# A fused decoder layer in fp32 split in two parts: packed order behind the chosen experts, a shared product ahead of the barrier, row numbers stored beside the routed tiles, another order of the attention steps

## The reference

```python
x = layernorm(x + attention(x))            # 16 heads of 32, causal, q k v and output projections with biases
x = layernorm(x + chosen(x, token_ids))    # 4 experts; the expert of a row is given by its token id:
                                           # y = (silu(x @ W[e].T) * (x @ W[e].T)) @ W[e].T, all three weights are ctx_2048
h = x @ Wr; probs = softmax(h); the two largest of 8 experts, weights not renormalised
moe = sum over the two of prob * (silu(x @ Wg[e]) * (x @ Wu[e])) @ Wd[e]          # F = 352
shared = sigmoid(x @ Wsg) * ((silu(x @ Sg) * (x @ Su)) @ Sd)                      # 1408 columns
out = layernorm(x + moe + shared)
```

## Time and profile before

| | |
|---|---|
| median of three runs | 1285.53 us (1281.93, 1285.53, 1288.90) |
| the profiled execution: its time, its span | 1281.12 us, 1279.4 us |
| PE busy, PEld busy | 1183.3 us (92%), 938.2 us (73%) |
| VectorE, ACT, GpSimd busy | 691.8 us (54%), 455.7 us (36%), 238.2 us (19%) |
| DMA | 169.72 MB, mean 133 GB/s |
| attention, until the first chosen load | 0 to 459.4 us |
| chosen experts | 459.4 to 597 us |
| routed phase | 597 to 1279.4 us |

### The profile page before, as it was taken

How to read it: one execution, slowest core, us unless ns; L and a number is a source line. 1 busy time by engine, 2 the same in 40 slices (tenths; PEclk the granted TensorE clock), 3 DMA queues, 4 the chain that set the end, 5 groups by cost and what they waited for, 6 DMA issues and landing times.

```text
span 1279.4 us, 20171 instructions
## 1 busy us (share of the span) xinstructions
PE 1183.3 (92%) x6404; PEld 938.2 (73%) x6404; DVE 691.8 (54%) x1469; ACT 455.7 (36%) x698; POOL 238.2 (19%) x358
## 2 busy tenths in 40 slices
PE   7788999999999769995999999999999999899996
PEld 5555566566576558884678888899999998678885
DVE  5664556656657546664547744444344432676754
ACT  3244334433435222221433334244444443333331
POOL 2021312412513410002300441000000000433200
PEclk8989999999999879997899999999999999999998
DMA  7355663532523322223523566344444531656440
GB/s 241 84 168 163 222 187 106 151 93 51 141 64 89 108 82 83 83 83 94 170 74 99 177 223 211 92 150 138 150 152 146 186 106 42 205 178 199 142 140 33
DMA packets 129276, 169.72 MB, mean 133 GB/s; under 512 B 17552, under 2 KB 70800, under 8 KB 129168
## 3 DMA queue, kind: packets, MB, share of 16 engines
q1 hardware_dynamic: 115360, 136.64, 34.7%
q0 software_dynamic: 8496, 28.32, 6.6%
q10 hardware_dynamic: 5312, 3.42, 1.1%
HBM read 95.98 MB, written 47.19 MB: 112 GB/s over the span
## 4 chain that ended last, share of the span: by engine, by line
PE 52%; DVE 4%; POOL 2%; issue 2%; DMA 2%; ACT 1%; SPq 0%; ACTq 0%; DVEq 0%; POOLq 0%
PE routed_ps L808 17%; PE routed_ps L1361 16%; PE chosen_psG L808 4%; PE chosen_psY L808 4%; PE routed_ps L1380 2%; PE routed_ps L1381 2%; PE routed_ps L1382 2%; POOL routed_rows_io L1299 2%; PE routed_ps L1402 1%; DVE routed_held L1704 1%; PE routed_ps L1425 1%; PE chosen_psX L889 1%; DMA routed_wdraw<-in_L_ffn_Wd_dram 1%; PE chosen_psH L908 1%; PE routed_ps L1326 1%
## 5 line engine op out<-in xcount | busy, mean ns | idle before, releaser
L459 PE MATMUL psT<-store 128*128 128x512 f32 x576 | 159.9, 412 | 5.1 <-DVE store L673 3.2
L742 DVE CUSTOM_DVE_ANT_0 psS<-psS,attn_mask 128x512 f32<-128x512 f32 (+3 forms) x256 | 120.6, 514 | 54.6 <-PE psS L525 54.5
L629 ACT ACTIVATE acc<-psE 128x512 f32<-128x512 f32 x160 | 92.9, 598 | 147.5 <-PE psE L546 143.5
L1361 PE MATMUL routed_ps<-routed_later,routed_held 128*128 128x512 f32 x528 | 124.7, 392 | 5.9 <-issue 2.9
L1361 PE MATMUL routed_ps<-routed_first,routed_held 128*128 128x512 f32 x528 | 127.6, 395 | 1.4 <-DVE routed_first L1800 1.4
L459 PEld LDWEIGHTS psT<-store 128*128 128x128 f32 x576 | 108.1, 198 | 26.0 <-issue 3.9
L1361 PEld LDWEIGHTS routed_ps<-routed_later,routed_held 128*128 128x128 f32 x528 | 98.3, 188 | 30.1 <-DVE routed_held L1704 6.6
L808 PE MATMUL routed_ps<-routed_held,routed_h_hi 128*128 x624 | 116.3, 328 | 0.6 <-DVE routed_h_lo L1745 0.6
L1361 PEld LDWEIGHTS routed_ps<-routed_first,routed_held 128*128 128x128 f32 x528 | 99.4, 190 | 22.1 <-DVE routed_first L1800 1.8
L1299 POOL DMA_INDIRECT routed_rows_io<-sorted_y,routed_pos x32 | 37.5, 1173 | 388.1 <-DMA sorted_y<-routed_rows_io 314.3
L402 POOL TENSOR_SCALAR_AFFINE_SELECT acc<-acc 128x256 f32<-128x256 f32 (+1 forms) x160 | 56.9, 361 | 282.8 <-ACT acc L629 281.9
(11 more groups left out here) (248 smaller groups left out, 1980.1 us busy)
## 6 DMA issues: line engine op xcount, KB each, us to landing
sorted_x<-attn_zero SPq DMA_DIRECT2D x19, 768.0 KB, 4.7
routed_sraw<-in_L_ffn_Sg_dram SPq DMA_DIRECT2D x44, 256.0 KB, 3.1
routed_sraw<-in_L_ffn_Su_dram SPq DMA_DIRECT2D x44, 256.0 KB, 3.6
routed_sraw<-in_L_ffn_Sd_dram SPq DMA_DIRECT2D x44, 256.0 KB, 3.9
routed_rows_io<-sorted_x SPq DMA_DIRECT2D x39, 256.0 KB, 2.9
sorted_y<-routed_rows_io SPq DMA_DIRECT2D x39, 256.0 KB, 2.2
attn_qS<-attn_ch_hi SPq DMA_DIRECT2D x128, 64.0 KB
attn_kS<-attn_ch_hi SPq DMA_DIRECT2D x112, 64.0 KB
```

The lines of the kernel that those rows point to most:

```text
L459: last = pe.matmul(out, lhs[a](k), rhs[c](k), start=(s[-1] == 0 and k == 0), stop=(s[-1] == 2 and k == KC - 1))
L629: act.activation(p_f[:, u, :], psE[:, n % 2, :], ACT.Exp, scale=SCALE).then_inc(exp_done, 1)
L742: last = dve.tensor_tensor_reduce(scores, scores, mask[:, (3 - t) * P:T], 1.0, BELOW_ALL, ALU.add, ALU.max, rowmax[:, g % 2, t, i:i + 1])
L1361: last = pe.matmul(out, w[:, slot, at + k * P:at + (k + 1) * P], x_part(k), start=(g == 0 and k == 0), stop=(g == 2 and k == KC - 1))
```

## The change

- The chosen experts' results are no longer gathered in token order but in packed order: position r of the packed order is the r-th row of the sorted rows without padding. RT3 works out three tables: packed (where packed row r lies among the padded rows), place (the packed position of each token) and, from an iota, number (the token's number).
- Twelve of the sixteen gathers are issued inside the chosen block, from tile 5 on. The input tiles of that block live in the last four tiles of acc, whose first loads SP issues before the barrier.
- The shared expert's weights, their semaphores and the PSUM banks belong to the whole kernel. The chosen block loads and splits chunks 0 and 1 and the router's weights, turns the first four tiles (front), and PE makes the shared product 0 with the last down product between its halves. ACT loads its Silu table at the start of that block.
- While the routed products run, GpSimd scatters the token numbers to their packed places in DRAM and loads them back as token. Output tiles are scattered by GpSimd to the rows in token; SP no longer stores them.
- In attention XT tiles of the next batch come earlier, P1 starts a slot later, the clears follow K only, the bias addition is cut into four, its last one with LN2, ST and LZ before it moves earlier, and GpSimd drains before the last PV steps.
- The other places of the diff pass names along, count constants or rename semaphores.

```diff
         b, at = s // 4, s % 4
-        fill = []
...
         if at == 1:
             turn = [("XT", b + 1, i) for i in range(QT)] if b + 1 < B else []
             out = [product("PR", b - 1, i) for i in range(QT)] if b else [[]] * QT
-            fill += turn[:2] + out[0] + out[1] + out[2] + turn[2:] + out[3]
+            fill += (out[0] + out[1] + out[2] + turn[2:] + out[3]) if b else []
+            early = turn[:2]
+            soon = [] if b else turn[2:]
...
         for n, one in enumerate(head):
-            steps += [one] + left[n:n + 1] + (p1[n - 2:n - 1] if n >= 2 else [])
+            if (s, n) == (1, 1):
+                steps += [("RT3",)]
+            steps += [one] + left[n:n + 1] + (p1[n - 3:n - 2] if n >= 3 else [])
             if n == 3:
...
             p1 = p1[2:]
         else:
-            p1 = p1[4:]
...
         if s:
             for n, j in enumerate(order):
-                steps += [("PV", s - 1, j)] + p1[n:n + 1] + p2[n:n + 1]
-                if n == 1 and at == 3 and b:
+                steps += [("PV", s - 1, j)] + p1[n:n + 1] + p2[n:n + 1] + early[n:n + 1]
+                if s == NG - 2 and n < 2:
+                    for i in (2 * n, 2 * n + 1):
+                        steps += [("LN2", b - 1, i), ("ST", b - 1, i)]
+                if s == NG - 1:
+                    steps += [("ZB", b, n)]
+                if n == 1 and at == 3 and b and b < B - 1:
                     steps += [("LZ", b)]
...
         steps += spread(slots, fill)
         if s:
             steps += [("YH", s - 1)]
-        if at == 2 and b:
+        if s == NG - 2:
+            steps += [("LZ", B - 1)]
+        elif at == 2 and b:
             for i in range(QT):
                 steps += [("LN2", b - 1, i), ("ST", b - 1, i)]
-        if at == 3:
-            steps += [("ZB", b)]
+        if at == 3 and b < B - 1:
+            steps += [("ZB", b, i) for i in range(QT)]
     b = B - 1
-    steps += [("PV", NG - 1, j) for j in order] + [("NH", 0), ("CW", 9), ("NH", 1)]
+    steps += [("DR",)] + [("PV", NG - 1, j) for j in order] + [("NH", 0), ("CW", 9), ("NH", 1)]
...
-                    if g >= 3:
-                        for _ in range(min(2, len(pieces))):
+                    if g >= 3 and qk == 1:
+                        for _ in range(min(4, len(pieces))):
                             clear()
...
             sp.wait_ge(x1_out, 16 * QT * B)
+            for s in range(4):
+                sp.dma_start(acc[:, NT - 4 + s, :], sorted_x1[s * P:(s + 1) * P, :]).then_inc(xs_in[s], 16)
...
-                    pool.tensor_tensor(z[:], z[:], bp[:].unsqueeze(1).broadcast_to([P, QT, C]), ALU.add).then_inc(zb_done, 1)
+                    pool.tensor_tensor(z[:, i, :], z[:, i, :], bp[:], ALU.add).then_inc(zb_done, 1)
...
+                elif kind == "RT3":
+                    then(dve.memset(start[:, 0:1], 0.0))
+                    for e in range(E):
+                        then(dve.tensor_tensor(start[:, e + 1:e + 2], start[:, e:e + 1], pre[:, NT, e:e + 1], ALU.add))
+                    then(dve.tensor_tensor(pad, base, start[:, 0:E], ALU.subtract))
+                    then(dve.tensor_tensor(step, pad[:, 1:E], pad[:, 0:E - 1], ALU.subtract))
+                    shape = [P, NT, E - 1]
+                    then(dve.tensor_tensor(beyond, full(iota_r, shape, 2), full(start[:, 1:E], shape, 1), ALU.is_ge))
+                    then(dve.tensor_tensor(beyond, beyond, full(step, shape, 1), ALU.mult))
+                    then(dve.tensor_reduce(picked1, beyond, AX, ALU.add))
+                    then(dve.tensor_tensor(picked1, picked1, iota_r, ALU.add))
+                    then(dve.tensor_copy(packed[:], picked1))
+                    then(dve.tensor_tensor(posf, posf, full(pad, [P, NT, E], 1), ALU.subtract))
+                    then(dve.tensor_tensor(picked, posf, sel, ALU.mult))
+                    then(dve.tensor_reduce(picked1, picked, AX, ALU.add))
+                    dve.tensor_copy(place[:], picked1).then_inc(place_done, 1)
+                    dve.wait_ge(place_done, 1)
...
+def shared_product(pe, weights, slot, x, outs, between=None):
+    KC = weights.width // (2 * P)
+    for m, out in enumerate(outs):
+        at = m * KC * P
+        for g, (w, x_part) in enumerate(((weights.hi, x[0]), (weights.hi, x[1]), (weights.lo, x[0]))):
+            for k in range(KC):
+                last = pe.matmul(out, w[:, slot, at + k * P:at + (k + 1) * P], x_part(k),
+                                 start=(g == 0 and k == 0), stop=(g == 2 and k == KC - 1))
+            if between:
+                between(3 * m + g)
+    last.then_inc(weights.up_full, 1)
...
+        SPLIT_AT = 6
+        FRONT_AT = 11
+        FRONT = weights.front_hi.shape[2] // P
+        turns = []
+        for s in range(NS):
+            turns.append(("x", s))
+            if FRONT_AT < s <= FRONT_AT + FRONT:
+                turns.append(("front", s - FRONT_AT - 1))
...
-            for s in range(4):
-                load_x(s)
             for s in range(NS):
+                if s == 1:
+                    weights.load(sp, 0, 0)
+                    for n, cols in ((0, slice(0, -1)), (1, slice(weights.wr_raw.shape[2] - 1, None))):
+                        sp.dma_start(weights.wr_raw[:, :, cols], router[n].rearrange("(k p) e -> p k e", p=P),
+                                     allow_slow_non_contiguous=True).then_inc(weights.small_in, 16)
+                    weights.load(sp, 1, 1)
...
                 pool.tensor_tensor(rstd[:, s % 2:s % 2 + 1], veps[:, s % 2:s % 2 + 1], powm[:, 0:1], ALU.pow).then_inc(rstd_done, 1)
+                if 5 <= s < NS - 2:
+                    t = s - 5
+                    for r in range(4):
+                        pool.wait_ge(stored[r], 16 * ((t + EXTRA - r + 4) // 4))
+                    pool.indirect_dma_start(out=acc[:, t, :], out_offset=None, in_=sorted_y[0:(t + EXTRA + 1) * P, :],
+                                            in_offset=bass.IndirectOffsetOnAxis(ap=packed[:, t:t + 1], axis=0)).then_inc(x2_of[t], 16)
...
                 turn_h(s)
-            down(NS - 1, was)
+                if ("front", s - FRONT_AT) in order:
+                    turn_front(s - FRONT_AT)
+            pe.wait_ge(weights.up_low, 1)
+            pe.wait_ge(x_low, len(turns))
+            shared_product(pe, weights, 0, [lambda k, x=x: x[:, k, :] for x in (weights.front_hi, weights.front_lo)], (bank[:, 0, :], bank[:, 2, :]),
+                           lambda g: down(NS - 1, was) if g == 2 else None)
...
+                if s in (SPLIT_AT, SPLIT_AT + 2):
+                    up = (slice(None), slot, slice(0, weights.width))
+                    dve.wait_ge(weights.up_high, slot + 1)
+                    dve.tensor_tensor(weights.lo[up], weights.raw[up], weights.hi[up].bitcast(F32), ALU.subtract).then_inc(weights.up_low, 1)
...
-            def store_out(t):
-                sp.wait_ge(out_done, t + 1)
-                sp.dma_start(out_dram[t * P:(t + 1) * P, :], acc[:, t, :]).then_inc(stored, 16)
...
-            for t in range(NT):
+            for t in range(NT - 4, NT):
                 pool.indirect_dma_start(out=acc[:, t, :], out_offset=None, in_=chosen_y,
-                                        in_offset=bass.IndirectOffsetOnAxis(ap=chosen_pos[:, t:t + 1], axis=0)).then_inc(x2_in[t if t < QT else QT - 1 + t // QT], 16)
+                                        in_offset=bass.IndirectOffsetOnAxis(ap=packed[:, t:t + 1], axis=0)).then_inc(x2_of[t], 16)
...
+            pool.wait_ge(x_turned, 4)
+            for t in range(NT):
+                pool.indirect_dma_start(out=token_rows, out_offset=bass.IndirectOffsetOnAxis(ap=place[:, t:t + 1], axis=0),
+                                        in_=number[:, t:t + 1], in_offset=None).then_inc(ids_out, 16)
+            pool.wait_ge(ids_out, 16 * NT)
+            pool.dma_start(token[:], token_rows.rearrange("(t p) a -> p (t a)", p=P), allow_slow_non_contiguous=True).then_inc(token_in, 16)
+            pool.wait_ge(token_in, 16)
...
+            def store_out(t):
+                pool.wait_ge(out_done, t + 1)
+                pool.indirect_dma_start(out=out_dram, out_offset=bass.IndirectOffsetOnAxis(ap=token[:, t:t + 1], axis=0),
+                                        in_=acc[:, t, :], in_offset=None).then_inc(stored, 16)
...
                     power(FINAL_AT[n], FINAL_AT[n])
-            for t in LAST:
+                    if FINAL_AT[n]:
+                        store_out(FINAL_AT[n] - 1)
+            store_out(LAST[0] - 1)
+            power(LAST[0], LAST[0])
+            for t in LAST[1:]:
                 power(t, t)
+                store_out(t - 1)
+            store_out(LAST[-1])
+            pool.wait_ge(stored, 16 * NT)
 
         @block.tensor
...
-            for t in range(QT):
-                turn(t)
-            pe.wait_ge(turn_low, QT)
-            shared_up(0, lambda g: turn(QT + g - 1) if 1 <= g <= QT else None)
+            turn(4)
+            turn(5)
```

(5 more changed lines are left out.)

286 lines of the change are left out of this document (169 added, 117 removed).

## The result

The kernel with the change takes 1276.9 us (median of 17 runs, 1269.9 to 1282.6) against 1281.8 for the kernel before on the same chip; the ratio is 0.9953, 95% interval 0.9931 to 0.9974. That is 5 us faster where I forecast 26, and outside my range. The profiled execution took 1270.9 us with a span of 1269.2, so span against span it is 10.2 us.

A forecast was written before the change was run, and what follows sets the result against it. TensorE, busy for 92% of the 1279.4 us span, was taken as the bound. The hole with its costs -19, attention -9.5 and tail +2 gave -26.5 from 1281.1, so 1254.6, put at 1256 us; range 1244 to 1270.

The forecast's parts named there:

- Hole, -22.0: Behind the chosen-expert stage: early gathers and an early shared product fill PE's idle time, 22.0 us less.
- Attention, -9.5: All attention changes together, from input transposes to the last batch's end: 9.5 us less (-16 to -3).
- XT, -5.8: In attention: next batch's input transposes moved into the PV steps cover PE's waits for rows and PSUM, 5.8 us less.
- the clears, -2.2: In attention: clears all after K let the K stack land earlier in two windows, 2.2 us less (-4.8 to 0).
- RT3: In attention: 16 small dependent VectorE operations, partly beside PE's products, cost 1 us (0 to +3.7).
- the bias sum: Last attention batch: bias additions cut in four and moved ahead, 1.5 us less (-4.2 to -0.3).
- the early loads: End of attention: the four first tiles' loads, issued before the barrier, shorten PE's wait by 1 us (-2.7 to 0).
- Sixteen scatters of row numbers: Routed phase: scatters and a load fit in GpSimd's 314.3 us wait; nothing, or up to +2 us crossing a weight load.
- Tail, +2: Kernel's end: the last two output stores, now on GpSimd, land later, 2 us more (+0.7 to +4).
- early work doesn't pay: Rival, chance 0.06: store waits hold GpSimd in the chosen stage and stop PE, about 15 to 20 us, 1275 to 1280.
- The rival of the stores: Rival, chance 0.04: output stores on GpSimd's queue hold the adding loop's gathers, up to 53 us in all, 1308.
- that of attention: Rival, chance 0.17: attention keeps its length, as other waits pin its windows; 1264, up to 1268 us.

The follow-up runs named there:

- xt_back: The changed kernel with the transposes of the next batch's input (XT tiles) back in the filling, as before the change; ratio 0.9991 to the kernel before.
- p1_back: The changed kernel with the P1 parts of attention one slot earlier again, as before the change; ratio 0.9893 to the kernel before.
- pad_32: The changed kernel plus an unused tensor of 32 bytes per partition, putting h_hi and h_lo back on a multiple of 64; ratio 0.9933 to the kernel before.
- late_product: The changed kernel with the first shared product back behind the barrier, as PE's first work of the last phase; ratio 1.0012 to the kernel before.

## Why the prediction was wrong

- **Hole, -22.0:** right; 22.0 from turn_h(18) to the steady products. I had charged 1 us for the clock; it stayed up, and PE never stood for more than 1.55 us there. The four turns in the chosen stage, +1.8: the stage grew by 2.1.
- **Attention, -9.5:** 7.9 in the two traces, with the spread of 8 us from execution to execution named above (451.1 to 459.4 in sixteen traces; the old order, 462.2 and 468.6). The total is right within that; of the parts, only XT and the P1 shift were taken out by a run, and the others are read off one pair of traces. XT, -5.8: right as a net, by xt_back; its first window alone went from 26.65 to 20.83 and the later two of its kind from 32.63 to 31.31 and from 32.56 to 31.34. Of the ten other windows behind the third M six grew by 0.2 to 0.9, some 2.7 in all over the ten, for which I had nothing; p1_back takes about 2 of it back. Of the clears, -2.2, half: -1.1 in the first of the two windows. RT3 seems under-priced: the window from the first to the second M grew by 4.5 us in the profiled execution, by 2.2 (p1_back) to 4.4 in the other kernels with it, for my +1; no run leaves RT3 out, and P1 moved in that window too. The end: -3.1 for the bias sum, for which I had -1.5, and -1.6 for the early loads, for which I had -1. The lines below, against the earlier trace rows, show where I was too careful: the subtraction of 4.64 us takes 0.42, PE's wait of 6.27 is 2.06, and GpSimd's masks hold the PV products for 0.78, where I had charged 1.5 to 3.7.

```profile
424.31 0.85 PE L587 MATMUL psO<-acc 128*32 128x384 f32 x8 [0.78 <-POOL acc L424]
...
429.28 0.42 DVE L816 TENSOR_TENSOR attn_yT_lo<-acc,attn_yT_hi 128x256 fp32r<-128x256 f32 x1 [0.47 <-ACT attn_yT_hi L663]
...
429.75 1.91 PE L482 MATMUL psT<-attn_wp_hi,attn_yT_hi 128*128 128x512 f32 x4 [2.06 <-DVE attn_yT_lo L816]
```

- **The failed step** is "Sixteen scatters of row numbers ... Nothing, or up to +2 where it crosses a weight load". It cost 12.1 us in the profiled execution, and 16.9 to 17.6 in the four others that keep the block as it is (pad_32, late_product, xt_back, p1_back), which show the freeze. That would also fit the median of the changed kernel, 6 us above its profiled execution; only one of its 17 executions has a trace. My cover was GpSimd's 314 us of idle time and the landing of 3.8 us. Both are true and beside the point: the price is paid by other engines. Packed 4-byte writes make the packets of SP's weight loads last 2.7 times as long, and beside a run of sixteen indirect transfers, 1.27 us apart, ScalarE and VectorE stand for 10 to 20 us in 13 of the 14 traces that have one, and PE with them, for 11.7 to 15.4 us where the run lies at the place of the changed kernel. What happens inside the chip in that stop no run shows.
- **Not foreseen:** the step of 8.24, 1.6 us in the first half, from 32 bytes of address, and probably most of the 1.5 us in the second (179.8 to 180.8 us in the four kernels with the pad, 180.8 to 182.0 in those without). New tensors ahead of h_hi, of sizes that are no multiple of 64, were in the diff.
- **Tail, +2:** right, +2.3. The stores did not hold the adding loop.
- The rivals: "early work doesn't pay" gave 1275 to 1280 and the kernel takes 1276.9, but not by its mechanism, so that match is luck; the chosen stage grew by 2.1 us only. Its sum was wrong, too: 15 to 20 us on 1254.6 are 1270 to 1275. And the forecast's upper bound, by my own terms (-12 - 3 + 4), is 1270 and not 1265. The rival of the stores and that of attention are out too. The case that came was on my list of costs, with the price of a transfer alone.

## What to carry to other kernels

Price a burst of indirect transfers by what it does to the queues and engines beside it, not by the issuing engine's idle time: keep small writes 64 bytes apart, keep runs short (each was seen to remove its effect; short runs alone, with the writes still packed, made it worse, 298.6 us, and the two together were not tried), and look in the trace for a DMA share near 1 at a low GB/s and for waits that nothing ends. When a change adds a tensor, compare the start addresses of what PE reads before and after. The fastest version found here that computes everything is the change with the run in the steady shared products and the pad, 1264.5 us, ratio 0.9821.

## What the hardware showed that I had not expected

- Sixteen scatters of 128 packed 4-byte rows: SP's packets take 0.207 us instead of 0.077 while they are in flight; with the same 4 bytes 64 bytes apart 0.075, with rows of 512 bytes 0.082. Gathers of 4-byte elements don't do it (0.068).
- A run of sixteen indirect transfers, scatter or gather, rows of 4 bytes to 2 KB: ScalarE stands for 11 to 20 us, in one to three pieces, with no releaser in the trace, until 0.4 to 3.1 us after the last is issued. Of the profiled executions with such a run only that of the changed kernel shows no such stop, with the slow loads alone. Runs of four and of three never did this.
- Matmuls with 512 moving columns whose stationary part lies in a tensor that starts 32 bytes past a multiple of 64: 0.2333 us apart; at a multiple of 64: 0.2267. With 352 moving columns no difference was seen.
